# Row masks of a two-layer graph attention made in layer 0 by ScalarE and stored, and layer 1's opening reordered

## The reference, cut to what matters

```python
# x (4096, 512), adj (4096, 4096), 8 heads of 64 in both layers
h = relu(layernorm(x))                       # layer 0
data1 = (h @ W.T + b).reshape(N, H, D)
e = leaky(src[h, n] + trg[h, m]) + adj[n, m]         # adj from 0 to 1e9
x = x + softmax(e, -1) @ data1
h = relu(layernorm(x))                       # layer 1
adj1 = maximum(adj, eye(n))
atts = einsum('hqk,hmk->hqm', h Wq, h Wk) / 8 - 1e16 * (1 - adj1)
x = x + einsum('hqm,hmk,hko->qo', softmax(atts, -1), h Wv, Wo)
```

## Time and profile before

| | us |
|---|---|
| median of 3 runs (lowest, highest) | 4701.43 (4700.53, 4702.29) |
| the profiled execution, its own time | 4695.88 |
| its span, first to last instruction | 4693.8 |
| layer 0, attention (first DVE product to last PE product) | 188.63 to 1623.35 |
| layer 1, projection | 1641.49 to 1962.84 |
| layer 1, attention: opening up to the first score | 1962.84 to 2053.07 |
| layer 1, attention: body up to the last product | 2053.07 to 4667.85 |

### The profile page before, as it was taken

How to read it: one execution, slowest core, us unless ns; L and a number is a source line. 1 busy time by engine, 2 the same in 40 slices (tenths; PEclk the granted TensorE clock), 3 DMA queues, 4 the chain that set the end, 5 groups by cost and what they waited for, 6 DMA issues and landing times. The chain is left out here.

```text
span 4693.8 us, 112624 instructions
## 1 busy us (share of the span) xinstructions
PE 4392.4 (94%) x42765; PEld 2123.5 (45%) x43276; DVE 3712.7 (79%) x7754; ACT 3079.7 (66%) x5766; POOL 3445.6 (73%) x2951
## 2 busy tenths in 40 slices
PE   8699999999999879689999999999999999999998
PEld 4222222222222234336556556555565565565554
DVE  5599999999998733387968878878778779788786
ACT  5355555555555433248778778778787787788786
POOL 2467777777777500049889989989889898899896
PEclk9899999999999989879999999999999999999999
DMA  4445544545442133453533433434425334334334
GB/s 152 120 123 159 149 129 155 156 133 150 145 149 87 62 123 114 128 165 95 153 108 94 149 100 109 142 87 127 127 85 150 103 101 150 109 99 151 92 111 128
DMA packets 425486, 583.02 MB, mean 124 GB/s; under 512 B 45376, under 2 KB 234176, under 8 KB 419456
## 3 DMA queue, kind: packets, MB, share of 16 engines
q1 hardware_dynamic: 420256, 560.13, 39.8%
q0 software_dynamic: 4576, 15.73, 1.2%
q10 hardware_dynamic: 128, 0.13, 0.0%
HBM read 499.02 MB, written 76.82 MB: 123 GB/s over the span
## 5 line engine op out<-in xcount | busy, mean ns | idle before, releaser
L1344 POOL TENSOR_TENSOR d_PL<-d_PF,d_PH 128x512 f16<-128x512 f32 x2048 | 2353.0, 1184 | 423.5 <-ACT d_PH L1389 419.9
L1446 DVE CUSTOM_DVE_ANT_0 d_junk<-d_gd,d_MR 128x512 bf16<-128x512 f32 x2112 | 1428.3, 686 | 381.1 <-issue 352.1
L1385 ACT ACTIVATE d_PF<-d_sc 128x512 f32<-128x512 f32 x2048 | 1279.2, 625 | 580.5 <-DVE d_sc L1533 380.0
L1389 ACT ACTIVATE d_PH<-d_sc 128x512 f16<-128x512 f32 x2048 | 1288.9, 629 | 0.0
L763 DVE SCALAR_TENSOR_TENSOR b_P<-R,u,b_A 128x512 f32<-128x512 f32 x1792 | 1195.2, 737 | 76.4 <-PE b_den L814 39.7
L807 PE MATMUL b_acc<-b_P,V 128*64 128x512 f32 x4096 | 947.8, 601 | 47.1 <-DVE b_P L763 33.8
L1575 PE MATMUL d_gd<-d_KA,d_QA 128*128 128x512 f16 x2112 | 817.4, 387 | 127.6 <-DVE d_gm L1446 76.5
L1591 PE MATMUL d_sc<-d_QA,d_KA 128*128 128x512 f16 x2048 | 777.1, 379 | 20.1 <-ACT d_PH L1389 15.8
L1592 PE MATMUL d_sc<-d_QL,d_KB 128*128 128x512 f16 x2048 | 776.3, 379 | 0.0
L1612 PE MATMUL d_acc<-d_V,d_PH 128*128 128x65 f16 x8192 | 639.2, 193 | 3.4 <-ACT d_oC L1367 1.3
L1614 PE MATMUL d_acc<-d_V,d_PH 128*128 128x64 f16 x8192 | 640.2, 193 | 0.0
(11 more groups left out here) (132 smaller groups left out, 4202.2 us busy)
## 6 DMA issues: line engine op xcount, KB each, us to landing
d_stage<-in_adj SPq DMA_DIRECT2D x288, 256.0 KB, 3.4
d_V<-scratch_v SPq DMA_DIRECT2D x131, 520.0 KB, 4.5
stage<-in_adjT SPq DMA_DIRECT2D x128, 512.0 KB, 5.2
b_rows<-in_adj SPq DMA_DIRECT2D x112, 512.0 KB, 4.3
d_MT<-scratch_mt SPq DMA_DIRECT2D x35, 1024.0 KB, 6.3
d_KA<-scratch_kh SPq DMA_DIRECT2D x272, 128.0 KB, 3.0
d_KA<-scratch_kl SPq DMA_DIRECT2D x272, 128.0 KB, 3.1
d_KB<-scratch_kh SPq DMA_DIRECT2D x264, 128.0 KB, 3.3
```

What stands on the lines that cost most here:

```text
L1344: eng.tensor_tensor(PL[:, t % H_RING, :], PF[:, t % F_RING, :], PH[:, t % H_RING, :], ALU.subtract).then_inc(s_lowp if by_pool(t) else s_l ...
L1385: nc.scalar.activation(PF[:, t % F_RING, :], sc[(nb * TILES + t) % BANKS][:, :], ACT.Exp, scale=EXP_SCALE)
L1389: nc.scalar.activation(PH[:, t % H_RING, :], sc[(nb * TILES + t) % BANKS][:, :], ACT.Exp, scale=EXP_SCALE).then_inc(s_P, 1)
L1446: nc.vector.tensor_tensor_reduce(out=junk[:, gi % 2, :], in0=gd[gi % 2][:, :], in1=MR[:, s, c * QB:(c + 1) * QB], scale=1.0, scalar=-3.0e3 ...
```

## The change

1. Row masks in layer 0. ACT gets its own stream. In each of the 256 steps it stores the piece made one step earlier, waits for the piece of adj that it asked for one step earlier, asks for the next, and makes one piece of 128 x 512 with an Identity activation (`mask_row`). A first piece of a block also waits for `s_lim`, the negated row limits `nlim`, which DVE makes after its step 0 of that block. The masks go to a new scratch tensor `mr` (bf16). To make room in memory, `STAGES` goes from 4 to 3, and so does the prefetch.
2. Layer 1 attention. `mask_chunk`, its staging ring and its loads go. SP loads each of the four rows of 128 x 4096 of `mr` (`load_mr`) as soon as the guards have used the one before (`ROW_FREE`), and DVE only rewrites the diagonal piece four steps later (`mask_diagonal`).
3. Layer 1 attention, opening. The fills of KB, QL and shift are made by POOL; DVE's low half of Wo stands after the guards; PE waits for constants only where it uses them.
4. Layer 1 projection. x is loaded ahead of POOL's fills; each weight has a semaphore of its own; weight 0 is split before the rest, weight 1 after the first turned h and weight 2 between the second and third product of group 0. PE no longer waits for all three. The hardware loops are written out.
5. Some semaphores are merged (`s_norm` into `s_chain`, `s_amax` into `s_rank`, `s_cmh` into `s_cm`, and others).

```diff
 layer0_attention
-    STAGES = 4
+    STAGES = 3
+    SW = N // 8
+    PIECES = SUB * N // SW
+    MASK_SCALE = 2.0 ** 58
...
+            def mask_row(nb, par, j):
+                n = nb * PIECES + j
+                if n:
+                    store_row(n - 1)
+                act.wait_ge(s_srow, 16 * (n + 1))
+                if n + 1 < NB * PIECES:
+                    load_row(n + 1)
+                if j == 0:
+                    act.wait_ge(s_lim, nb + 1)
+                if n >= 2:
+                    act.wait_ge(s_mr, 16 * (n - 1))
+                s = j // (N // SW)
+                nc.scalar.activation(mrow[:, n % 2, :], srow[:, n % 2, :], ACT.Identity, bias=nlim[:, par, s:s + 1],
+                                     scale=MASK_SCALE).then_inc(s_ms, 1)
...
                     if m + SIGN_AHEAD < NT:
                         sign(nb, m + SIGN_AHEAD, first)
+                    mask_row(nb, par, m)
...
+                    if m == 0:
+                        if nb:
+                            dve.wait_ge(s_rank, nb * (CHUNKS + 1))
+                            dve.wait_ge(s_ms, nb * PIECES - PIECES)
+                        nc.vector.tensor_scalar(nlim[:, par, :], T["amax"][:, nb * SUB:(nb + 1) * SUB], 1.0, -MASK_SCALE,
+                                                ALU.max, ALU.mult).then_inc(s_lim, 1)
 layer1_project
-            with eng.Fori(0, NB - 1) as g:
-                body(g, False)
-            body(NB - 1, True)
+            for g in range(NB):
+                body(g, g == NB - 1)
...
+                if g == 0:
+                    low_weights(1)
                 for j in range(PAIRS):
+                    if g == 0 and j == 2:
+                        low_weights(2)
 layer1_attention
-            for ci in range(S_RING, CHUNKS):
-                sp.wait_ge(s_mk, chunk_done(ci - S_RING))
-                load_chunk(sp, 0, ci)
...
+                        for s in range(SUB):
+                            if step == ROW_FREE[s]:
+                                sp.wait_ge(s_gm, (nb * HP + HP - 1) * GUARDS + 2 * MC * (s + 1))
+                                load_mr(sp, (nb + 1) % NB, s)
...
+            pool.memset(QL[D:P, :, :, :], 0.0).then_inc(s_fill, 1)
+            pool.memset(KB[D:P, :, :], 0.0).then_inc(s_fill, 1)
```

More of the change, by code:

```diff
@@ L664, in exp_adj @@
                     act.wait_ge(s_P, nb * (NT * HV) + (m - A_RING + 1) * HV)
[L665 removed]
+                tile = stage[:, (nb * LOADS + m // PAIR) % STAGES, m % PAIR, :]
                 nc.scalar.activation(A[m % A_RING][:, :], tile, ACT.Exp).then_inc(s_exp, 1)
@@ L919, in _ @@
             pool.memset(vt[:, :, :, D:D + 1], QK_SCALE).then_inc(s_vset, 1)
-            pool.sem_inc(s_h, SUB)
-            with pool.Fori(0, NB) as g:
+            for g in range(1, NB):
                 for s in range(SUB):
-                    wait_apart(pool, s_h, g * SUB + (s + 1), s_passed)
-                    pool.dma_start(xg[:, s, :], DR["x1"][bass.ds(g * QB + s * P, P), :]).then_inc(s_x[s], 16)
+                    pool.wait_ge(s_h, (g - 1) * SUB + (s + 1))
+                    load_x(g, s)
         @block.vector
@@ L947, in _ @@
             aggregate(0)
+            low_weights(0)
             norm(0)
-            for i in range(3):
-                dve.wait_ge(s_wh, i + 1)
-                nc.vector.scalar_tensor_tensor(out=WS[i][:, 1, :, :], in0=W[i][:, :, :], scalar=W_SCALE, in1=WS[i][:, 0, :, :],
-                                               op0=ALU.mult, op1=ALU.subtract).then_inc(s_ws, 1)
             def body(g, last):
@@ L1109, in guards_of @@
         return range(upto(mb - 1), upto(mb))
-    FIRST_C = (HP - 2) * NT + 12
-    CHUNK_STEPS = [FIRST_C + 5 * ci // 4 for ci in range(CHUNKS)]
-    SETUP_STEP, DIAG_STEP = FIRST_C - 1, FIRST_C - 9
-    S_USES = [(CHUNKS + S_RING - 1 - i) // S_RING for i in range(S_RING)]
+    ROW_FREE = [(HP - 2) * NT + next(m for m in range(NT) if 2 * MC * (s + 1) - 1 in guards_of(m)) + 1 for s in range(SUB)]
+    DIAG_STEP, SETUP_STEP = (HP - 2) * NT + 1, (HP - 2) * NT + 6
+    ROW_SET = [free + 4 for free in ROW_FREE]
     POOL_SLOTS = (0, 1, 2, 3)
@@ L1185, in layer1_attention @@
         s_MT = [sem(f"mask_in{i}") for i in range(GROUPS)]
-        s_stage = [sem(f"adj_in{i}") for i in range(S_RING)]
+        s_MR = [sem(f"mask_rows_in{s}") for s in range(SUB)]
         s_dblk = sem("adj_diagonal_in")
@@ L1261, in _ @@
             load_diagonals(sp, 0)
-            for ci in range(S_RING):
-                load_chunk(sp, 0, ci)
+            for s in range(SUB):
+                load_mr(sp, 0, s)
             for hp in range(2):
@@ L1339, in _ @@
                 sp.wait_ge(s_MT[i], 16 * (NB + (1 if i < GROUPS - 1 else 0)))
+            for s in range(SUB):
+                sp.wait_ge(s_MR[s], 16 * (NB + 1))
         def split(eng, engine, nb, t):
@@ L1537, in body @@
                                 row = gi // (2 * MC) + 1
-                                count = nb * MASK_OPS + (MASK_OPS + 2 + ROW_OPS * row) if hp == HP - 1 and gi % (2 * MC) == 0 else None
+                                count = nb * MASK_OPS + (MASK_OPS + 2 + row) if hp == HP - 1 and gi % (2 * MC) == 0 else None
                                 guard(nb * HP + (hp + 1), gi, count)
@@ L1543, in body @@
                             mask_setup(nb + 1, (nb + 1) % NB)
-                        for ci in range(CHUNKS):
-                            if step == CHUNK_STEPS[ci]:
-                                mask_chunk(nb + 1, (nb + 1) % NB, ci)
+                        for s in range(SUB):
+                            if step == ROW_SET[s]:
+                                mask_diagonal(nb + 1, (nb + 1) % NB, s)
             for nb in range(NB):
@@ L1718, in build @@
             T["am"] = sb0("am0", [P, 2, QB])
-            T["stage"] = sb0("stage0", [P, 4, 2, QB])
+            T["stage"] = sb0("stage0", [P, 3, 2, QB])
             T["s_am"] = layer0.enter_context(nc.semaphore("am_in0"))
             T["s_R"] = layer0.enter_context(nc.semaphore("r_in0"))
-            T["s_stage"] = [layer0.enter_context(nc.semaphore(f"adjT_in{i}")) for i in range(4)]
+            T["s_stage"] = [layer0.enter_context(nc.semaphore(f"adjT_in{i}")) for i in range(3)]
             layer0_project(nc, T, DR)
```

200 lines of the change are left out of this document (105 added, 95 removed).

## The result

| | before | changed |
|---|---|---|
| median of five runs each, same chip | 4702.29 us (4700.53 to 4702.96) | 4677.22 us (4674.02 to 4679.12) |
| ratio of the two, 95% interval | | 0.9949 (0.9938 to 0.9960) |
| profiled execution, span | 4695.88, 4693.8 us | 4677.40, 4675.6 us |
| busy PE, DVE, ACT, POOL | | 95, 76, 69, 73% of the span |

The change gains **25 us** by the medians, within the range that was given and under half of the 55 us that were forecast. First the windows by stage of the changed kernel; columns as in the earlier trace rows. The cuts are PE's own here: first matmul and last of layer 0's attention, the projection's first turn, its last product, the first score, the last product.

What follows compares the result with a forecast made beforehand. Prediction: PE near its pace in both attentions except layer 1's opening and mask chunks; terms -58 + 22 + 4 - 12 - 11 = -55 us, giving 4641 on the profile, 4646 us by the median; range 4621 to 4692.

Steps and rivals of the forecast that it cites:

- Layer 1, body, -58: Layer 1 attention body: removing mask chunks gains 58 us of the 70.5 paid around them; 1.5 us a block remain.
- the 79 that were named as a sign against the term: Layer 1 body: hp 2 and hp 3 over 79 us would show the body term wrong; near 77.5 right.
- the rival's mechanism: Layer 1 body: diagonal pieces and setup all delay PE, gain 29 instead of 58 us, total 4675; chance 0.13.
- Layer 0, block starts, +22: Layer 0 attention: mask pieces ahead of the b_oT copies in ACT's queue cost 3.2 us at seven block starts, +22 us.
- Layer 0, loads, +4: Layer 0 attention: later row pieces and added DMA traffic cost 0.5 us a block, bounds 0 and 4, +4 us.
- layer 0's loads get in each other's way: Layer 0, R and row pieces: +4 us a block, 28 more, total about 4675 to 4690; chance 0.08.
- The ring of three, 0: Layer 0 stage loads: three places leave POOL two steps (11 us) against a landing of 5.2 us; no cost.
- Projection, -12: Layer 1 projection: earlier x load and weight 0 split first start PE's first turn earlier, -12 us, bounds -8 to -13.
- Opening, -11: Layer 1 attention opening: first score comes earlier, -11 us (-8 to -13), with 5 MB queued ahead of the keys.
- The slower rival: Layer 0: ACT paced by its piece loads if landing exceeds 5.1 us; at 5.8, 180 us added, 4826; chance 0.08.
- its two signs: Layer 0, ACT paced by its loads: ACT idle on b_srow in most steps, and blocks over 184 us.

Runs made afterwards that it cites:

- ahead: Changed kernel, with ACT issuing each step's mask-piece store and load right behind its exponential, one semaphore per buffer place; 4673.61 us, ratio to before 0.9929.
- late_ahead: Changed kernel, with mask pieces of steps 0 to 15 one step later, behind the copies, and their DMAs issued behind ACT's exponential; 4645.67 us, ratio to before 0.9867.
- ring3: Kernel before, with only layer 0's ring of stage places and prefetch at 3 instead of 4; 4711.82 us, ratio to before 1.0019.
- no_piece_loads: Changed kernel without 254 of ACT's 256 loads of adj pieces, pieces made with scale 0, so row masks left out; 4665.35 us, ratio to before 0.9921.
- rows_first: Changed kernel, with SP asking for the next block's first two row pieces ahead of the eight R loads; 4668.19 us, ratio to before 0.9928.
- combined: Changed kernel with pieces one step late, their DMAs behind the exponential, row pieces ahead of R, opening keys early and fills on ACT; 4606.22 us, ratio 0.9795.
- opening2: Changed kernel, with q and first keys loaded behind the first mask row alone, each diagonal piece made just before its row's guards; 4668.79 us, ratio to before 0.9929.
- unrolled: Kernel before, with only the hardware loops of layer 1's projection written out; 4703.31 us, ratio to before 0.9995.

## Why the prediction was wrong

Between the profiled executions the difference is -18 us where -55 was forecast: block starts +37.4, the rest of layer 0's attention +14.0, first turn of the projection -11.1, the rest of it +2.1, opening -8.7, body -54.2, and +2 at the two ends of the span. Of the 37 us that are missing, 15 are the block starts' and 10 the loads'.

- **Layer 1, body, -58: the size right, partly by luck.** -54.2; 14.2 us are left where 12 were counted. The way there was another. The prediction spread the residue over hp 2 and hp 3 and had DVE's spare time swallow most of 5.2 us a block. The program puts all of it in hp 2, which takes 79.5 us, over the 79 that were named as a sign against the term; hp 3 takes 76.7. The diagonal pieces cost 0.37 us each, not 1.04, the setup 2.1 us a block, not 1: 3.6 us of DVE in all, and hp 2 is 2.3 us longer for it, 1.8 of that in the one wait behind the setup. So the residue was smaller than counted and most of it was paid: the rival's mechanism, with another size. That moving the setup away from the output's two instructions would free these 1.8 us is not tested.
- **Layer 0, block starts, +22: the mechanism right, the size wrong; this is one of the two steps that failed.** PE waits 36.9 us in seven waits, 24.8 more than before; the forecast 3.2 x 7 is 22, and of the 24.8 it is the order in ACT's queue that gives 22.4 (`ahead`), the late start of DVE the rest. The prediction took the wait for the whole price ("the 2.8 to 3.7 us are lost in full"). PE's clock falls in it, and the steps lose another 12.6 us: 37.4. Shown by `ahead` against `late_ahead`.
- **Layer 0, loads, +4: the other failed step.** 14 us. "0.5 a block" was taken near the lower bound of 0 to 4, because PE had not noticed such waits before. The ring alone costs 7.7 (`ring3`), the loads 11 (`no_piece_loads`), and the order of R and the row pieces can give 7.5 to 9 of it back (`rows_first`); the three overlap. In block 0's step 4 two waits lie over each other, DVE's for the rows behind R and ACT's for its own load: `rows_first` alone leaves 2.8 of the 6.0 us and `late_ahead` 2.3, `combined` none. The rival "layer 0's loads get in each other's way" had the cause, with 32 us where 14 came. The Trainium skill's rule on issuing engines (DMA: Bandwidth & Descriptors, Issuing engines are not separate DMA queues), which the prediction weighed and set aside, pointed to this: row pieces land in 6.6 us instead of 4.3 and R in 9.6 instead of 8.7 over this stage. Not all of that is ACT's: with the shorter ring alone they land in 5.3 and 8.9, without ACT's loads in 5.9 and 9.0.
- **The ring of three, 0:** +9 us by the ratio of `ring3`. POOL nearly has its two steps: it waits 4.9 us in all for `stage`, in four waits. What was overlooked is that `load_r` is issued at pair `STAGES`, so R moved too, and in block 0 the first row pieces are asked for 1.3 us later against PE's start. That this is what the 7.7 us are was not taken apart.
- **Projection, -12: nearly right.** The first turn comes 11.1 us earlier. It stands 16.3 us after x is asked for (forecast 15.5):

```profile
1699.32 1.91 ACT L1056 ACTIVATE c_wqS<-c_wq 128x2048 f16<-128x2048 f32 x1 [20.33 <-DMA c_wq<-in_Wq]
...
1708.13 2.92 ACT L1051 ACTIVATE c_h<-c_xg,c_nmr,c_rstd 128x512 f32<-128x512 f32 x4 [0.83 <-DVE c_nmr L997]
...
1711.11 3.68 PE L1105 MATMUL c_tp<-identf,c_h 128*128 128x128 f32 x16 [23.64 <-ACT c_h L1051]
```

  From there to the last product it is 294.4 us against 292.3; of the kernels with this projection some have 292.2 and some 294.5, so that is no effect of the change.
- **Opening, -11: a little less**, -8.7, at the weak end of its bounds, for the reason the prediction named (5 MB ahead of the keys): PE waited for the first keys until 2033.79, 28 us behind the projection's last product. POOL's fills hold DVE up as well, which it did not see; that stayed hidden here, and came to light in `opening2`.
- **The slower rival** (ACT paced by its loads) did not come, though the loads land in 5.0 us, close to the 5.1 from which it was to decide. Of its two signs one is absent (ACT waits for a load in 69 steps of 256). The other is there, blocks over 184 us (184.6 to 187.0 in blocks 1 to 6), but by the block starts: without ACT's loads they are 183.0 to 185.2. ACT waits 178 us for loads, most of it where nobody waits for ACT; at a block's end somebody does.
- **The two measures.** The profiles differ by 18 us, the medians by 25. The profiled run of before was 6.4 us under its median; its body took 2614.7 us, that of `unrolled` and `ring3`, with the same code there, 2621.2 and 2620.6. So the body's gain of 54.2 us rests on a pair of profiles of which each could have been some 6 us longer.

## What to carry to other kernels

A wait of PE costs its length only while the clock stays up: count what comes behind a longer wait at both levels, and look at the granted clock of the window before calling a gap small. When work is added to an engine that has time "by block", look at the two ends of the block: ahead of the copies that others wait for there is no slack, and a DMA wait in the last steps travels round through the engines that work ahead. A loss that is cured at one step can come back at the next wait that it hid: step 4 went from 9 to 17 us when the steps 0 were cured, until the rows went ahead of R. Here the same work, placed one step later, with its DMAs asked for a few instructions earlier and the row pieces ahead of R, turned +51 us in that stage into -7.5.
